# A fused two-layer kernel: the units' second products three half ticks behind the first

## What is computed

```
x = x + tanh(g_xattn[0]) * L0_xattn(layernorm(x), ctx, ctx, ...)   # attention over 16 heads, within a token
x = x + tanh(g_ffn[0])   * L0_ffn(layernorm(x), ...)               # 2 of 8 experts by a rule, relu
x = x + tanh(g_xattn[1]) * L1_xattn(layernorm(x), ctx, ...)        # vision-language attention, 64 x 64
x = x + tanh(g_ffn[1])   * L1_ffn(layernorm(x), ...)               # the part that the change touches
```

```
scores = softmax(xt @ gate_w.T)
_, idx = top_k(scores + gate_bias, 2)
for e in range(8):
    gate_e = sum(where(idx == e, weights, 0))
    h = silu(xt @ w1[e].T) * (xt @ w3[e].T)
    y = y + gate_e * (h @ w2[e].T)
z = silu(xt @ sw1.T) * (xt @ sw3.T) @ sw2.T                        # shared, 256 wide
```

## Time and profile before

| | |
|---|---|
| time, median of 3 runs | 1388.08 us (1386.64 to 1390.91) |
| the profiled execution's own time | 1374.39 us |
| its span, first to last instruction | 1372.6 us |
| busy: PE, PE weight loads, DVE, ACT, POOL | 82%, 70%, 75%, 43%, 46% |
| granted TensorE clock, mean | 0.92 |

### The profile page before, as it was taken

The page is one execution under the profiler, slowest core; times in us unless marked ns, Lnnn a source line. Parts: engine busy times, 40 slices in busy tenths (PEclk is TensorE's granted clock), DMA queues, the critical chain, the costliest instruction groups (busy, mean ns, idle before and its releaser), DMA issues.

```text
span 1372.6 us, 23593 instructions
## 1 busy us (share of the span) xinstructions
PE 1122.3 (82%) x7464; PEld 961.7 (70%) x7464; DVE 1026.4 (75%) x2393; ACT 587.4 (43%) x1506; POOL 637.2 (46%) x377
## 2 busy tenths in 40 slices
PE   4244446999879996997989999998888888988887
PEld 2133324888768985886878989887777767777776
DVE  2999999989999999985364444447777777777766
ACT  2211212656446553654536454543334443443332
POOL 4889989898789979893301101011111111111000
PEclk9965555999979997999899999999999999999999
DMA  6101114988478965895561555510000000000000
GB/s 214 46 24 38 38 47 155 276 277 255 151 231 281 280 216 171 258 296 180 183 199 53 180 167 184 164 30 21 18 24 24 21 19 24 24 24 24 8 8 16
DMA packets 125036, 166.41 MB, mean 121 GB/s; under 512 B 10033, under 2 KB 67569, under 8 KB 124913
## 3 DMA queue, kind: packets, MB, share of 16 engines
q1 hardware_dynamic: 119792, 152.31, 35.9%
q0 software_dynamic: 5120, 12.59, 2.8%
HBM read 137.60 MB, written 27.26 MB: 120 GB/s over the span
## 4 chain that ended last, share of the span: by engine, by line
PE 55%; DVE 24%; issue 8%; POOL 6%; ACT 3%; SPq 2%; DMA 1%; DVEq 0%; POOLq 0%; ACTq 0%
PE ZB L1274 9%; PE YB L1288 6%; PE YD L1325 4%; DVE q_sb L896 4%; PE ZD L1242 3%; PE ZD L1244 3%; PE ZD L1243 3%; DVE s L871 3%; POOL prod L585 3%; PE ZD L1288 2%; PE YB L1325 2%; DVE hu L1094 2%; PE MC L1238 2%; POOL xs L595 2%; PE MA L1233 2%
## 5 line engine op out<-in xcount | busy, mean ns | idle before, releaser
L561 POOL TENSOR_TENSOR rstd<-ve,neghalf 128x4 f32<-128x4 f32 x64 | 65.7, 1026 | 581.3 <-DVE ve L825 580.9
L682 ACT ACTIVATE hid<-ZB,w2b 128x128 f32<-128x128 f32 x768 | 215.6, 377 | 163.5 <-PE YB L1288 81.5
L573 POOL TENSOR_TENSOR prod<-q_sb,kv_sb 128x2048 f32<-128x2048 f32 x48 | 216.3, 4508 | 53.4 <-DVE q_sb L896 33.3
L585 POOL TENSOR_TENSOR prod<-s,kv_sb 128x2048 f32<-128x2048 f32 x48 | 215.3, 4507 | 7.5 <-DVE q_sb L896 7.5
L1274 PE MATMUL ZB<-bt,w1b 128*128 128x128 f32 x1536 | 212.5, 284 | 1.2 <-ACT hid L682 0.9
L1274 PEld LDWEIGHTS ZB<-bt,w1b 128*128 128x128 f32 x1536 | 196.7, 200 | 4.0 <-issue 3.4
L704 ACT ACTIVATE own_prod<-ZD 128x512 f32<-128x512 f32 x102 | 61.1, 599 | 232.5 <-PE ZD L1244 230.9
L1288 PE MATMUL YB<-w2b,hid 128*128 128x128 f32 x1024 | 141.0, 281 | 0.0
L1288 PEld LDWEIGHTS YB<-w2b,hid 128*128 128x128 f32 x1024 | 128.5, 194 | 14.7 <-ACT hid L682 9.0
L1094 DVE TENSOR_TENSOR hu<-own_prod,ZD 128x512 f32<-128x512 f32 x102 | 69.8, 684 | 72.8 <-ACT own_prod L704 45.4
L1109 DVE SCALAR_TENSOR_TENSOR own_prod<-YD,gate,own_prod 128x128 f32<-128x128 f32 x320 | 89.9, 343 | 30.4 <-PE YD L1325 27.8
(11 more groups left out here) (250 smaller groups left out, 2335.0 us busy)
## 6 DMA issues: line engine op xcount, KB each, us to landing
w2b<-in_w SPq DMA_DIRECT2D x96, 516.0 KB
w1b<-in_w SPq DMA_DIRECT2D x96, 512.0 KB, 4.9
xb<-xs SPq DMA_DIRECT2D x96, 128.0 KB, 3.4
ctx_t<-in_ctx SPq DMA_DIRECT2D x32, 256.0 KB, 2.9
x2d<-x2s SPq DMA_DIRECT2D x48, 128.0 KB, 5.2
x<-in_x SPq DMA_DIRECT2D x16, 256.0 KB, 3.8
xs<-zrow SPq DMA_DIRECT2D x4, 1024.0 KB, 10.6
xrow<-in_x SPq DMA_DIRECT2D x16, 256.0 KB, 3.9
```

Of the source, the lines that this page charges most:

```text
L573: pool.tensor_tensor(out=prod[:, t % 2, :].rearrange("p (h e d) -> p h e d", h=HEADS, e=HEADS), in0=q.unsqueeze(2).broadcast_to([P, HEADS, ...
L585: pool.tensor_tensor(out=prod[:, (t + 1) % 2, :].rearrange("p (h d e) -> p h d e", h=HEADS, e=HEADS), in0=s0[:, t, :, :].unsqueeze(2).broa ...
L682: act.activation(hid[n % 2][:, j, k * RT:(k + 1) * RT], ZB[j // 2][:, at:at + RT], ACT.Relu, bias=w2b[t % 3][:, k, e, FJ * D + j:FJ * D + ...
```

## The change

The second product of a unit, and its sum, come three half ticks behind the first product instead of two: out u and in u + 2 now fall in the same half tick for u from 1 to 7. `hu` gets three buffers, which lie in a part of `prod` that is free by then, so `unit_gated` waits for the second product three units back; the pieces of the weights that are split at the start go through `vk_t` and `lk_t` instead of `hu`. GpSimd's `norm(3)` moves from pos 14 to 12, ScalarE's `normed(3)` from 15 to 13, TensorE's `xt3` from 15 to 14; `ut_hi` stays in 15, `ut_lo` moves from 15 to 16 (which is pos 0 of the next period), `lg` from 16 to 17, `logits_max` from 16 to 18. `ut_hi` and `ut_lo` have two buffers each. `route_tokens` and the exp of the logits stay where they are.

The turn of the banks changes with the order of issue: lk MA, lg MC, xt2 MA, vk MC, then as before. So `xt2` now fills the bank that `lk` had, and `vk` the bank that `lg` had.

```diff
--- before.py
+++ after.py
@@ -83,11 +83,11 @@
 
 
 UNIT_IN = {1: 0, 2: 1, 4: 2, 5: 3, 7: 4, 8: 5, 10: 6, 11: 7, 13: 8, 14: 9}
-UNIT_OUT = {pos + 2: u for pos, u in UNIT_IN.items()}
-
-
-C_FIRST = {0: "lk", 1: "vk", 2: "vv", 4: "bdt"}
-C_LATER = {0: "xt2", 1: "sc", 4: "val", 5: "att", 7: "xt3"}
+UNIT_OUT = {pos + 3: u for pos, u in UNIT_IN.items()}
+
+
+C_FIRST = {0: "lk", 1: "vk", 2: "vv", 4: "bdt", 7: "xt3"}
+C_LATER = {0: "xt2", 1: "sc", 4: "val", 5: "att"}
 
 
 def a_part(half):
@@ -153,7 +153,7 @@
     for half in range(2 * TICKS):
         tick, later = half // 2, half % 2
         order = [(None, "bt", t) for t in sorted_next(half) if tick >= CROSS] + tail_uses(half)
-        if not later:
+        if later:
             order += [(None, "lg", d) for d, k in d_parts(tick) if k == 0]
         stages = C_LATER if later else C_FIRST
         order += [(None, stages[k], c) for c, k in c_parts(tick) if k in stages]
@@ -301,8 +301,9 @@
 
 
         xn3 = prod[:, 0, 0:CH].rearrange("p (j d) -> p j d", j=TILES)
-        ut_hi, ut_lo = sb("ut_hi", [P, CH], F32R), sb("ut_lo", [P, CH], F32R)
-        su, hu = own_prod[:, CH:3 * CH].rearrange("p (i n) -> p i n", i=2), sb("hu", [P, 2, CH])
+        ut_hi, ut_lo = ([sb(f"{n}{i}", [P, CH], F32R)[:] for i in range(2)] for n in ("ut_hi", "ut_lo"))
+        su = own_prod[:, CH:3 * CH].rearrange("p (i n) -> p i n", i=2)
+        hu = [prod[:, 0, i * CH:(i + 1) * CH] for i in range(1, 4)]
         xd = own_prod[:, 3 * CH:4 * CH].rearrange("p (j d) -> p j d", j=TILES)
         lg_sum, lg, sc1, scg, bs1, gate = (sb(n, [P, TILES, E1]) for n in ("lg_sum", "lg", "sc1", "scg", "bs1", "gate"))
         lmx, lsum, lrec = (sb(n, [P, TILES]) for n in ("lmx", "lsum", "lrec"))
@@ -311,7 +312,7 @@
 
         stats, mv23 = sb("stats", [P, 4, TILES, 6]), sb("mv23", [P, 2, TILES, 2])
         ve, nmean, rstd, nmr = (sb(n, [P, 4, TILES]) for n in ("ve", "nmean", "rstd", "nmr"))
-        raw = [hu[:, i, :] for i in range(2)]
+        raw = [vk_t[:], lk_t[:]]
 
         M = [bank("MA"), bank("MC")]
         ZB, YB = [bank("ZB0"), bank("ZB1")], bank("YB")
@@ -616,7 +617,7 @@
                     for c, kc in c_parts(tick):
                         if kc == -1:
                             norm(2, c)
-                        if kc == 7:
+                        if kc == 6:
                             norm(3, c)
                 if k == 4 and has(p):
                     norm(0, p)
@@ -700,7 +701,7 @@
             def unit_silu(d, u):
                 act.wait_ge(pe_up.sem, pe_up.at(d, u + 1))
                 if d * UNITS + u >= 2:
-                    act.wait_ge(hu_s.sem, hu_s.at(d, u - 1))
+                    act.wait_ge(hu_s.sem, d * UNITS + u - 1)
                 act.activation(su[:, u % 2, :], unit_pair[PAIR[d, u][0]][0][:], ACT.Silu).then_inc(silu_s.sem, 1)
 
             act.wait_ge(s_g, 32)
@@ -775,14 +776,15 @@
                             normed(2, lambda j: xn2[:, j, :], lambda j: x2[c % 2][:, j, :], c)
                         if kc == 0:
                             plain(xt2[:], "xt2", c)
-                        if kc == 7:
+                        if kc == 6:
                             if has(c - 1):
                                 filled(act, "xt3", c - 1)
                             normed(3, lambda j: xn3[:, j, :], lambda j: x3[:, j, :], c)
+                        if kc == 7:
                             b = filled(act, "xt3", c)
-                            if has(c - 1):
-                                act.wait_ge(pe_gate.sem, pe_gate.at(c - 1))
-                            act.activation(ut_hi[:], b[:], ACT.Copy).then_inc(ut_hi_s.sem, 1)
+                            if has(c - 2):
+                                act.wait_ge(pe_gate.sem, pe_gate.at(c - 2))
+                            act.activation(ut_hi[c % 2], b[:], ACT.Copy).then_inc(ut_hi_s.sem, 1)
                 for d, kd in d_parts(tick):
                     if 2 * kd + later in UNIT_IN:
                         unit_silu(d, UNIT_IN[2 * kd + later])
@@ -1087,11 +1089,10 @@
             def unit_gated(d, u):
                 dve.wait_ge(silu_s.sem, silu_s.at(d, u + 1))
                 dve.wait_ge(pe_gate.sem, pe_gate.at(d, u + 1))
-                if u >= 2:
-                    dve.wait_ge(pe_f.sem, pe_f.at(d, max(1, u - 2)))
-                elif has(d - 1):
-                    dve.wait_ge(pe_f.sem, pe_f.at(d - 1, E1 + u))
-                dve.tensor_tensor(out=hu[:, u % 2, :], in0=su[:, u % 2, :], in1=unit_pair[PAIR[d, u][0]][1][:], op=ALU.mult).then_inc(hu_s.sem, 1)
+                old = d * UNITS + u - 3
+                if old >= 0:
+                    dve.wait_ge(pe_f.sem, pe_f.at(old // UNITS, max(1, old % UNITS)))
+                dve.tensor_tensor(out=hu[(d * UNITS + u) % 3], in0=su[:, u % 2, :], in1=unit_pair[PAIR[d, u][0]][1][:], op=ALU.mult).then_inc(hu_s.sem, 1)
 
             def unit_sum(d, u):
                 if u == 0:
@@ -1182,6 +1183,10 @@
                         dve.tensor_tensor(out=lo, in0=raw[i % 2], in1=ZB[i % 2][:], op=ALU.subtract).then_inc(raw_lo.sem, 1)
                     for d, kd in d_parts(tick):
                         if kd == 0:
+                            dve.wait_ge(ut_hi_s.sem, ut_hi_s.at(d))
+                            b = filled(dve, "xt3", d)
+                            dve.tensor_tensor(out=ut_lo[d % 2], in0=b[:], in1=ut_hi[d % 2].bitcast(F32), op=ALU.subtract).then_inc(free_of("xt3", d), 1)
+                        if kd == 1:
                             logits_max(d)
                     for c, kc in c_parts(tick):
                         if kc == -2:
@@ -1204,10 +1209,6 @@
                             biased(BLV, u_sb, "val", c)
                         if kc == 5:
                             residual3(c)
-                        if kc == 7:
-                            dve.wait_ge(ut_hi_s.sem, ut_hi_s.at(c))
-                            b = filled(dve, "xt3", c)
-                            dve.tensor_tensor(out=ut_lo[:], in0=b[:], in1=ut_hi[:].bitcast(F32), op=ALU.subtract).then_inc(free_of("xt3", c), 1)
                     for d, kd in d_parts(tick):
                         unit_half(d, 2 * kd + 1)
 
@@ -1302,7 +1303,7 @@
                     elif pair == 1:
                         pe.wait_ge(relu_s.sem, relu_s.at(2 * NPAIRS - 1))
                     ns = slice((2 * u + i) * P, (2 * u + i + 1) * P)
-                    three(unit_pair[pair][i][:], w13_hi[:, ns], w13_lo[:, ns], ut_hi[:], ut_lo[:]).then_inc(done.sem, 1)
+                    three(unit_pair[pair][i][:], w13_hi[:, ns], w13_lo[:, ns], ut_hi[d % 2], ut_lo[d % 2]).then_inc(done.sem, 1)
 
             def unit_out(d, u):
                 if u == 0:
@@ -1320,9 +1321,9 @@
                     js = slice(j * P, (j + 1) * P)
                     if u == 1:
                         for v in range(SHARED):
-                            last = pe.matmul(b[:, js], hu[:, v, js], w2u_sb[:, v, :], start=(v == 0), stop=(v == SHARED - 1))
+                            last = pe.matmul(b[:, js], hu[(d * UNITS + v) % 3][:, js], w2u_sb[:, v, :], start=(v == 0), stop=(v == SHARED - 1))
                     else:
-                        last = pe.matmul(b[:, js], hu[:, u % 2, js], w2u_sb[:, u, :], start=True, stop=True)
+                        last = pe.matmul(b[:, js], hu[(d * UNITS + u) % 3][:, js], w2u_sb[:, u, :], start=True, stop=True)
                 last.then_inc(pe_f.sem, 1)
 
             def unit_half(d, pos):
@@ -1380,8 +1381,8 @@
                     for j in range(TILES):
                         js = slice(j * P, (j + 1) * P)
                         cols = slice(2 * j * E1, 2 * (j + 1) * E1)
-                        pe.matmul(b[:, cols], ut_hi[:, js], wg_parts[:], start=True, stop=False)
-                        last = pe.matmul(b[:, cols], ut_lo[:, js], wg_high[:], start=False, stop=True)
+                        pe.matmul(b[:, cols], ut_hi[c % 2][:, js], wg_parts[:], start=True, stop=False)
+                        last = pe.matmul(b[:, cols], ut_lo[c % 2][:, js], wg_high[:], start=False, stop=True)
                     last.then_inc(done, 1)
                 if name == "lk":
                     pe.wait_ge(ld_cc.sem, ld_cc.at(c))
```

## The result

The changed kernel takes **1375.93 us** (median of 5 runs, 1374.04 to 1380.41) against 1387.93 (1386.57 to 1390.91, 5 runs) for the kernel before on the same chip: ratio 0.992 (95% interval 0.9896 to 0.9945), a gain of 12.0 us. The forecast was a gain of 20.1 us, to 1368.0; the time is inside the range of 1357 to 1382. The profiled execution took 1379.39, of which 1377.7 is the span.

What follows compares the result with a forecast made beforehand. No engine was full; the late period was taken to run through ScalarE's normed rows, VectorE's route and back. Gains of 11.1 + 4.0 + 4.1 + 0.9 = 20.1 us, from 1388.1, gave 1368.0 us, range 1357 to 1382.

Steps and rivals of the forecast that it cites:

- The chain of a late period: Four legs between TensorE's starts from vv to the next vv: 36.6 us after, a gain of 1.1 us per period.
- rival B: Late periods: the waits come back in full and only the gains at the ends stay, 1379 us; chance 0.14.
- D: Whole kernel: the change does nothing because the chain is elsewhere, 1388 us; chance 0.05.
- C: Late periods slower: ScalarE's two table loads lie on the chain, 2.57 us a period, 1394 us; chance 0.06.
- A: Late periods: all holes close and TensorE alone bounds them at 31.4 us, 1316 us; chance 0.03, halfway 0.12.
- The ends and the gap: Behind the last chunk's att 4.0 us gained; in the gap between expert blocks 4.1, between 0 and 6.
- the new holes of 2.6 us are hardly longer than the 2.53 that passed at full clock: TensorE's late waits, at bdt after and out 3 before: the new holes were not expected to lower the clock.
- the whole 11.1: Late periods, vv of chunks 5 to 15: ten periods at 1.1 us gained each, 11.1 us in all.
- the earlier trace's low clock: TensorE from 672 to 676 us at 0.57 of full clock: costed at nothing; 1.7 us back should it vanish.
- The stretch of rows 2 with experts gets nothing: From 740 to 870 us, TensorE busy 129.28 of 130: no gain, new waits lie under expert products.
- The two rules of the Trainium skill: ScalarE: a drain of about 1380 ns follows each table load; TensorE: headroom read from weight loads, 28% and not 15%.
- the estimate of 31.4 for the work alone: TensorE in a late period: work without holes takes 31.4 of 37.7 us; four holes cost 6.2.

Runs made afterwards that it cites:

- the last version: The changed kernel with route_tokens moved behind score_parts and logits_max moved to the next half tick, ahead of sum 9 and gated 0: 1319.20 us.
- the filled kernels: Ten spare matmuls ahead of bdt's wait in the changed kernel (1363.50 us), or ahead of out 3's hu wait in the kernel before (1375.12 us).
- the second execution of before: The kernel before, unchanged, profiled once more: median 1387.96 us, ratio 1.0016, span of this profile 1386.2.

## Why the prediction was right, and where it was not

**The chain of a late period: right.** By the starts printed above, `vv` to `bdt` is 10.26 us (forecast 10.4), `bdt` to `att` 6.82 at full clock (6.8), `att` to `xt3` 6.73 (6.7), `xt3` to `vv` 12.52 (12.7): 36.3 against 36.6. The holes are 2.2, 1.1 to 1.4 and 1.0 to 1.5 against 2.6, 1.3 and 1.3, with the names forecast, and those for `hu` are gone. The time, 1375.9, is 0.9 us outside the band that was called the forecast (1361 to 1375), between it and rival B's 1379, but B's mechanism (the waits come back in full) isn't what happened: the late chain is 1.3 us a period shorter. D falls with it, and so does C, for the wait at `bdt` stayed under 4 us, and the table loads are no longer than in the earlier trace rows. A's 1316 is nearly reached by the last version (1319.2), yet not by this change: it took the route and the logits out of the way, and the period is then 33.7 and not A's 31.4.

**The ends and the gap: right within an us or two.** The two chunks around the gap gained 4.1 to 5.0 us (forecast 4.1), and the `unit_sum` wait there is 0.95; that the `x2s` wait near 677 us grew from 0.9 to 3.2 was not forecast, so the 4.1 is in part luck. Last `vv` to the end gained 2.7, with two falls of the clock after and one before (forecast 4.0; 4.2 between the filled kernels, 63.7 to 59.5).

**Failed: "the new holes of 2.6 us are hardly longer than the 2.53 that passed at full clock."** Behind eight of ten holes of 2.2 us it did not pass; each cost 1.6 us. Measured against the profile that was shown, this takes nearly the whole 11.1. It does little harm to the forecast only because the kernel before pays about as much in its usual execution (the fillers gained 13 to 15 and 11 to 12 us), and that is luck. I started from the median, rightly as it came out, but knew no reason for the 13.7 us between it and the profile. Of the earlier trace rows's low clock I had asked whether it vanishes; it is there still: from 668 to 692 us the granted clock is 0.79 before and 0.86 after.

**Failed: "The stretch of rows 2 with experts gets nothing."** It lost 5.1 us for two chunks (7.3 against the profile shown), and the next chunk lost 2.2 where 0.9 of gain was forecast. The step that failed is the search for cover: I followed the waits of TensorE's unit and cross products through the reordering, and put the expert products down as cover for all of them. That the experts' own `x2s` stands in the same queue of VectorE, behind route, sum 1 and gated 3, was not followed. The earlier trace rows showed TensorE busy 129.28 of 130 us there, so by that execution there was nothing to gain and any later `x2s` could only cost. (In the second one the norm shift had 1.15 us a chunk to gain, at `xt3`.)

The account, against the second execution of before: gap 4.1, late periods 10.3, end 2.7, make 17.1; experts and the chunk behind them take 7.3, and the start, ahead of nearly all that the change touches, 1.3: 8.5 between these two executions, 12.0 between the medians. That the start alone differs by up to 4.5 us between the profiles of the table is why a table of single profiles is not closed to the last us.

**The two rules of the Trainium skill.** In the kernel after no pause shows behind a table load either (ScalarE, start, length, what; below). By the Trainium skill's "ScalarE: Activation LUTs", What ACT_TABLE_LOAD costs, a drain should follow each load. This trace disagrees:

```profile
1127.53 1.28 ACT L762 ACT_TABLE_LOAD   x1
1128.82 0.23 ACT L762 ACTIVATE lg<-lg 128x32 f32<-128x32 f32 x1
```

In the kernel after the weight loads are busy 224.6 of 301.5 us. By the Trainium skill's "Perfetto Trace Analysis", Identifying the Most-Contended Engine, headroom is judged by them, which would leave 26%. The fastest kernel took a period from 37.7 to 33.7 us and then had TensorE busy 94% with the loads at 80%; in the estimate of 31.4 for the work alone a further 2.3 us are left. No run here got as far as that 26%.

## What to carry to other kernels

When a step is moved past a wait, follow every queue to its end, that of other work in the same stretch too: where TensorE is full (129.28 of 130 us here), a reordering has little to gain and can cost, and the long block that nobody waits for (here the route, 3.3 us on VectorE) sets the time of all that stands behind it. Move that block first; only then does distance between first and second products pay (5 to 6 us lost became 35 gained). And when the profiled execution lies 1% off the median, find out which stretch differs before a mechanism is read from it.

## What the runs showed of the hardware

Whether TensorE's clock falls behind a hole is not settled by the hole's length: 2.53 us in the same kernel passed at full clock ten times of eleven in one execution and four times of eleven in another; 2.23 and 2.25 us in one execution went either way. Behind a single late hole of 1.6 us or less no fall shows in any profile here, behind two (1.61 and 1.50 us, 0.5 us apart) one shows in each of ten periods. A fall cost 1.5 to 1.6 us. Spare matmuls in the hole kept the clock at 1.00 in the late part and gained 11 to 15 us in either kernel, though they did no work. What decides between holes of one length was not tried.
